# One store queue and seven v buffers in the first stage of a convolution and attention network (one core, fp32)

## The reference, cut to what matters

```python
g = group_norm(x)                         # 32 groups of 4 channels, per image
xn = g / (norm(g) * 128 ** -0.5 + 1e-8)   # simple_rms, per token
u = silu(xn @ W_u.T + b_u)                # made in a later stage, from the stored xn
v = silu(xn @ W_v.T + b_v)                # 256 channels: made and stored in the first stage
out = (u * conv2d_by_fft(v)) @ W_o.T + b_o + g
return x + out
```

## Time and profile before

| | |
|---|---|
| median of 3 runs | 3128.38 us (3125.18 to 3130.5) |
| the profiled execution, its own time | 3134.22 us |
| its span | 3132.4 us |
| busy in the span | TensorE 91%, VectorE 62%, ScalarE 40%, GpSimd 27% |
| moved | 315.48 MB, 101 GB/s mean |
| first stage over the images | about 21 to 331 us of the span |
| in that stage from 61 us on | TensorE busy 205.8 of 270 us, DMA share 0.77, 216 GB/s, mean granted TensorE clock 0.80 |

### The profile page before, as it was taken

One profiled execution on the slowest core, in us unless ns is written; L12 is line 12 of the kernel. 1 busy time (PEld: TensorE's weight loads), 2 busy tenths in 40 slices (PEclk: granted clock), 3 DMA queues, 4 the chain that ended last, 5 costly groups with the idle time before them and its releaser, 6 DMA issues. The chain is left out here.

```text
span 3132.4 us, 145347 instructions
## 1 busy us (share of the span) xinstructions
PE 2862.5 (91%) x62769; PEld 2113.4 (67%) x62769; DVE 1933.0 (62%) x3276; ACT 1262.5 (40%) x2841; POOL 843.7 (27%) x921
## 2 busy tenths in 40 slices
PE   5778798999999999999999979679999999999889
PEld 4555248966666666666666634348888888888779
DVE  4444353366666666666666657557778887778533
ACT  3555344332222222222222244356666666666300
POOL 0000002012222222222222212225555555555410
PEclk9778698999999999999999999889999999999999
DMA  5778100012112111212121199546666667666556
GB/s 139 213 211 231 53 1 1 0 31 46 45 44 46 44 46 44 46 44 46 44 46 44 43 366 400 228 80 104 106 102 99 100 105 107 102 103 98 80 142 199
DMA packets 839362, 315.48 MB, mean 101 GB/s; under 512 B 671729, under 2 KB 824878, under 8 KB 835118
## 3 DMA queue, kind: packets, MB, share of 16 engines
q1 hardware_dynamic: 503186, 176.24, 23.9%
q10 hardware_dynamic: 321692, 130.88, 15.8%
q0 software_dynamic: 14336, 6.45, 3.7%
HBM read 157.66 MB, written 155.75 MB: 100 GB/s over the span
## 5 line engine op out<-in xcount | busy, mean ns | idle before, releaser
L845 DVE TENSOR_TENSOR terms<-spec,ps_z 112x456 f32<-112x456 f32 x1024 | 575.0, 623 | 404.3 <-PE ps_z L728 404.3
L738 PEld LDWEIGHTS ps_q<-inv_w,prod 112*57 112x57 f32 x16384 | 450.9, 133 | 174.5 <-issue 172.2
L826 POOL TENSOR_TENSOR prod<-terms 112x456 f32<-112x456 f32 x256 | 297.6, 1162 | 1000.5 <-DVE terms L845 1000.5
L738 PE MATMUL ps_q<-inv_w,prod 112*57 112x56 f32 x16384 | 484.4, 217 | 1.2 <-DVE prod L851 1.2
L783 ACT ACTIVATE q_half<-ps_q 121x448 f32<-121x448 f32 x255 | 139.2, 546 | 827.1 <-PE ps_y L746 827.1
L728 PE MATMUL ps_z<-x_half,fwd_w 120*112 120x456 f32 x1024 | 458.4, 570 | 0.0
L1135 POOL TENSOR_TENSOR k_blocks<-k_mixed,same_of 128x896 f32<-128x896 f32 x112 | 188.1, 1680 | 398.2 <-ACT k_mixed L1301 398.2
L1152 POOL DMA_DIRECT2D v_blocks<-v_heads x448 | 272.7, 615 | 41.7 <-PE ps_o L1222 23.5
L728 PEld LDWEIGHTS ps_z<-x_half,fwd_w 120*112 120x112 f32 x1024 | 160.4, 176 | 122.0 <-issue 106.1
L1222 PE MATMUL ps_o<-p_norm,v_blocks 128*64 128x64 f32 x6272 | 213.4, 227 | 26.5 <-DVE p_norm L1386 23.6
L1222 PEld LDWEIGHTS ps_o<-p_norm,v_blocks 128*64 128x64 f32 x6272 | 197.4, 141 | 36.0 <-DVE p_norm L1386 29.8
(11 more groups left out here) (136 smaller groups left out, 4505.7 us busy)
## 6 DMA issues: line engine op xcount, KB each, us to landing
qk_heads<-st_qk ACTq DMA_DIRECT2D x56, 476.0 KB
qk_rows<-qk_heads SPq DMA_DIRECT2D x112, 238.0 KB
conv_in<-v_sb ACTq DMA_DIRECT2D x112, 224.0 KB, 3.3
v_in<-conv_in SPq DMA_DIRECT2D x512, 49.0 KB
conv_out<-y_sb ACTq DMA_DIRECT2D x512, 49.0 KB
y<-conv_out SPq DMA_DIRECT2D x8, 1792.0 KB, 13.2
x_in<-in_x SPq DMA_DIRECT2D x8, 1568.0 KB, 9.5
shortcut<-short ACTq DMA_DIRECT2D x8, 1568.0 KB, 6.2
```

Source lines behind the costliest of these rows:

```text
L738: last = pe.matmul(ps_q[64 * ri:64 * ri + NF, c * SIDE:(c + 1) * SIDE], prod[b % 2][:, x, c * NF:(c + 1) * NF], k.inv_w[:, x, ri * SIDE:(r ...
L826: pool.tensor_tensor(prod[b % 2][:, 1, :], terms[b % 2][:, 2, :], terms[b % 2][:, 3, :], ALU.add).then_inc(prod_i_r, 1)
L845: last = dve.tensor_tensor(terms[b % 2][:, x, :], k.spec[0:NFFT, s, bass.ds(c * CC, CC), :].rearrange("p c f -> p (c f)"), ps_z[b % 2][z][ ...
```

## The change

It is made in `project_in`, and one number in `attend`.

- `v_sb` gets NCH = 7 buffers in place of 2, one for each chunk of an image, with seven semaphores `v_stored`. The SiLU of chunk c of image b waits until the stores of chunk c of image b - 1 have landed.
- ScalarE issues no DMA in the stage any more. SyncE issues them all, loads and stores, from a program without a loop, in the order: loads 0, 1, 2; `short` of image 0; load 3; then for each image b the 14 stores of v, the store of `xr`, the store of `short` of image b + 1, and the load of image b + 4. Each waits for the same data as before; the load of image b still waits for image b - 2 to be turned.
- The increments of `aligned` ahead of TensorE's loop in `attend` go from 81 to 83.

TensorE's and VectorE's code in the stage is unchanged. The diff (the parts that only rename are in it too):

```diff
--- before.py
+++ after.py
@@ -218,7 +218,7 @@
         sq = [sb(f"x_sq{n}", [128, COLS]) for n in range(2)]
         rt, rt_eps, rinv = sb("rt", [TT, NCH * TPC]), sb("rt_eps", [TT, NCH * TPC]), sb("rinv", [TT, NCH * TPC])
         ROWS = COLS // SIDE
-        v_sb = [sb(f"v_sb{n}", [128, 2, ROWS, SIDE]) for n in range(2)]
+        v_sb = [sb(f"v_sb{n}", [128, 2, ROWS, SIDE]) for n in range(NCH)]
         gs = GroupStats(ctx, nc, "gn0")
         ps_ss = psum("ps_sumsq")
         ps_t, ps_bc, ps_v = ([psum(f"{n}{m}") for m in range(2)] for n in ("ps_turn", "ps_bcast", "ps_v"))
@@ -227,7 +227,8 @@
         sq_ready, ss_ready, rt_ready, eps_ready = sem("sq_ready"), sem("ss_ready"), sem("rt_ready"), sem("eps_ready")
         rinv_ready, bc_ready, xr_ready = sem("rinv_ready"), sem("bc_ready"), sem("xr_ready")
         v_ps_ready, v_ready, copies_read = sem("v_ps_ready"), sem("v_ready"), sem("copies_read")
-        v_stored, xr_stored, short_stored = ([sem(f"{n}{m}") for m in range(2)] for n in ("v_stored", "xr_stored", "short_stored"))
+        xr_stored, short_stored = ([sem(f"{n}{m}") for m in range(2)] for n in ("xr_stored", "short_stored"))
+        v_stored = [sem(f"v_stored{n}") for n in range(NCH)]
         block = ctx.enter_context(nc.Block())
 
         def cols(c):
@@ -248,13 +249,36 @@
 
         @block.sync
         def _(sp):
-            with sp.Fori(0, BATCH // 2) as i:
-                for a in range(2):
-                    b = i * 2 + a
-
-                    sp.wait_ge(x_turned, b * NCH + NCH)
-                    src = t.x_rows[bass.ds(b * TOK, TOK), :]
-                    sp.dma_start(x_in[a][:], src.rearrange("(a p) c -> p a c", p=TT)).then_inc(x_loaded[a], 16)
+            def load(b):
+                sp.wait_ge(x_turned, b * NCH + NCH)
+                sp.dma_start(x_in[b % 2][:], t.x_rows[b * TOK:(b + 1) * TOK, :].rearrange("(a p) c -> p a c", p=TT)).then_inc(x_loaded[b % 2], 16)
+
+            def store_short(b):
+                sp.wait_ge(short_ready, (b + 1) * NCH)
+                sp.dma_start(t.S[b], short[b % 2][:]).then_inc(short_stored[b % 2], 16)
+
+            def store_v(b, c):
+                sp.wait_ge(v_ready, (b * NCH + c) * 2 + 4)
+                for h in range(2):
+                    dst = t.V[b, c * ROWS:(c + 1) * ROWS, h * 128:(h + 1) * 128, :]
+                    sp.dma_start(dst.rearrange("r c w -> c r w"), v_sb[c][:, h]).then_inc(v_stored[c], 16)
+
+            def store_xr(b):
+                sp.wait_ge(xr_ready, b * NCH + NCH + 1)
+                sp.dma_start(t.XR[b], xr[b % 2][:]).then_inc(xr_stored[b % 2], 16)
+
+            for b in range(3):
+                load(b)
+            store_short(0)
+            load(3)
+            for b in range(BATCH):
+                for c in range(NCH):
+                    store_v(b, c)
+                store_xr(b)
+                if b + 1 < BATCH:
+                    store_short(b + 1)
+                if b + 4 < BATCH:
+                    load(b + 4)
 
         @block.tensor
         def _(pe):
@@ -295,27 +319,19 @@
         def _(act):
             act.sem_inc(x_copied, 2)
             act.sem_inc(v_ready, 2)
+            for n in range(NCH):
+                act.sem_inc(v_stored[n], 32)
             for n in range(2):
-                act.sem_inc(v_stored[n], 32)
                 act.sem_inc(xr_stored[n], 16)
                 act.sem_inc(short_stored[n], 16)
 
             def body(b, a, turn, norm, project):
                 def silu(c):
-                    n = (a * NCH + c) % 2
-
-                    act.wait_ge(v_stored[n], (b - a) * (NCH * 16) + ((a * NCH + c) // 2 + 1) * 32)
+                    act.wait_ge(v_stored[c], b * 32 + 32)
                     for h in range(2):
                         act.wait_ge(v_ps_ready, (b * NCH + c) * 2 + h + 1)
-                        act.activation(v_sb[n][:, h].rearrange("p r w -> p (r w)"), ps_v[h][:, 0:COLS], ACT.Silu,
+                        act.activation(v_sb[c][:, h].rearrange("p r w -> p (r w)"), ps_v[h][:, 0:COLS], ACT.Silu,
                                        bias=k.bias[:, 2 + h:3 + h]).then_inc(v_ready, 1)
-
-                def store(c):
-                    n = (a * NCH + c) % 2
-                    act.wait_ge(v_ready, (b * NCH + c) * 2 + 4)
-                    for h in range(2):
-                        dst = t.V[bass.ds(b, 1), c * ROWS:(c + 1) * ROWS, h * 128:(h + 1) * 128, :]
-                        act.dma_start(dst.rearrange("b r c w -> c (b r) w"), v_sb[n][:, h]).then_inc(v_stored[n], 16)
                 if turn:
                     act.wait_ge(copies_read, b + 3)
                 for c in range(NCH + 2):
@@ -328,23 +344,17 @@
                         act.wait_ge(xg_ready, (b + 1) * NCH + c + 1)
                         act.wait_ge(ss_ready, (b + 1) * NCH + c + 1)
                         act.activation(sq[c % 2][:], xg[1 - a][:, cols(c)], ACT.Square).then_inc(sq_ready, 1)
-                    if c > 1 and project:
-                        store(c - 2)
                 if turn:
                     gs.on_scalar(act, b + 2)
                 if norm:
                     act.wait_ge(ss_ready, (b + 2) * NCH + 2)
                     act.activation(rt[:], ps_ss[0:TT, 0:NCH * TPC], ACT.Sqrt, scale=1.0 / CH).then_inc(rt_ready, 1)
-                    act.wait_ge(short_ready, (b + 2) * NCH)
-                    act.dma_start(t.S[bass.ds(b + 1, 1)].rearrange("b p t -> (b p) t"), short[1 - a][:]).then_inc(short_stored[1 - a], 16)
-                if project:
-                    act.wait_ge(xr_ready, b * NCH + NCH + 1)
-                    act.dma_start(t.XR[bass.ds(b, 1)].rearrange("b p t -> (b p) t"), xr[a][:]).then_inc(xr_stored[a], 16)
             images(act, body)
             for n in range(2):
                 act.wait_ge(xr_stored[n], 16 * (BATCH // 2 + 1))
                 act.wait_ge(short_stored[n], 16 * (BATCH // 2 + 1))
-                act.wait_ge(v_stored[n], 32 * (BATCH * NCH // 2 + 1))
+            for n in range(NCH):
+                act.wait_ge(v_stored[n], 32 * (BATCH + 1))
 
         @block.vector
         def _(dve):
@@ -1238,7 +1248,7 @@
                     outputs(i - 1, (j - 1) % RING)
 
 
-            for _ in range(81):
+            for _ in range(83):
                 pe.sem_inc(aligned, 1)
             for w in range(AU):
                 for x in range(2):
```

## The result

The kernel after takes **3101.13 us** (median of 4 runs, 3099.78 to 3101.67), the kernel before 3127.45 us (4 runs, 3125.18 to 3130.5). The ratio is 0.9914, with a 95% interval of 0.99 to 0.9928: 26.3 us less. 3094.7 was forecast, with a range of 3083 to 3109. The profiled executions differ by 32.6 us in their spans, 3132.4 and 3099.8; of that 31.4 lie in the first stage, whose successor issues its first load at 300.34 in place of 331.72 us, and 1.2 behind it.

A forecast was written before the change was run, and what follows sets the result against it. TensorE was taken as the bound inside bodies, paying in full for ScalarE's store wait once per image. Gains of 31.3 (waits) + 2.4 (last body) = 33.7 us against the median 3128.4 gave 3094.7 us, range 3083 to 3109.

The forecast's parts named there:

- The waits: At the first stage's body ends, TensorE's waits for `rinv` fall from 47.3 to 16.0 us, a gain of 31.3 us.
- All in one queue: All first-stage transfers on SyncE's queue: 29.5 us an image with a load, 22.6 without; price 0.
- v: 3.21 MB at 219 GB/s: Time for one image's v stores in the first stage's queue: 14.7 us.
- The queue just keeps up: SyncE's queue keeps pace with the first stage's bodies; a store may be a whole body late unfelt; price 0.
- the last body's step: The first stage's data ends near +29.1 us from the last body's start; gain 2.4 us, ends 0 and 3.7.
- second rival: One queue is slower than two, v at 181 GB/s, 10 us paid behind the last body: 3105 us, chance 0.10.
- 7 us of a body's 30: SyncE's 17 issues of about 0.4 us in each first-stage body; price 0.
- The clock: TensorE's clock still falls around each first-stage body's end, so each body still pays about 4 us.
- first rival: TensorE's clock stays up in the first stage, bodies about 25.4 us, queue the bound: 3073 us; chance, wholly or partly, 0.12.
- none late: Bound on the clock term: TensorE's clock comes back late in none of the first-stage bodies, -4 us.
- falling up to 3 us into a body: Bound on the clock term: TensorE's clock falls only that far into a first-stage body, -5 us over six.
- bad loop: The loop in `attend` lies badly and TensorE waits 33 times: 39 to 109 us less 33.7, upper 3204 us, chance 0.05.

The follow-up runs named there:

- e1: The kernel before with seven v buffers and nothing else, ScalarE still issuing all stores: 3122.17 us, ratio 0.9985.
- e2: The kernel after with two v buffers again, all stores still on SyncE: 3127.53 us, ratio 0.9995.
- e3: The kernel after without the stores of `short` for images 1 to 7: 3089.08 us, ratio 0.9884.
- e5: The kernel after with `conv_in` laid out as image, channel, row, column, so v is stored in runs of 1792 bytes: 3084.24 us, ratio 0.9868.
- e7: The kernel after with 81 increments of `aligned` in place of 83: 3103.98 us, ratio 0.9931.
- e4: The kernel after with the stores of `xr` and `short` issued by ScalarE on its own queue: 3102.49 us, ratio 0.9928.
- e9: The kernel after with the second half of each chunk of v stored by ScalarE on its own queue: 3092.88 us, ratio 0.9889.

## Why the prediction was right, and where it was not

*The waits.* Right in size, and in mechanism for the two parts together. 16.0 us were to remain behind the first start's 1.7, 15.8 do: 2.1 to 2.2 at the ends of bodies 0 to 5, 2.8 at body 6. The step "What is late next is the roots' table load behind the last SiLU" is what the timeline after shows.

*The parts' shares.* The forecast never split the gain between the buffers and the move, and its wording, in which the SiLU "waits for stores of the image before", made the buffers the cause. e1 and e2 show that alone they are worth 3.8 us and the move nothing. The reading of the earlier trace rows was wrong by the issue of 3.87 us: it stood in the trace before, ahead of the SiLU, and the prediction counted the issues only as the 1.20 us ahead of the table load.

*All in one queue: the step that failed.* "v: 3.21 MB at 219 GB/s" is the top of a pulse of two or three stores, not a pace; kept busy the queue moves 187. The measured need is 25.4 to 25.7 us for an image without a load, where 22.6 were put, and 32.1 (183.97 to 216.07) with one, where 29.5 were. "The queue just keeps up" is wrong: bodies of 28.4 to 29.6 us are shorter than 32.1, it fell behind, and the stage paid for it behind the last SiLU, 23.9 us to the next load in place of the 8 that the last body's step gives. It is the second rival's mechanism, with its 181 GB/s, and as that rival said, no SiLU ever waited for it. e3 and e5 show it from two sides: with less in the queue, or the same in larger runs, the end comes 13.6 and 16.8 us earlier. The issues cost more than "7 us of a body's 30" too, 19 to 29 us of SyncE's time for the 14 stores of a body, but nothing waited for SyncE itself.

*The clock.* It fell around the ends of bodies 0 to 5 with only 2.2 us of rest there, as was argued from the earlier trace rows, so the first rival is out as a whole. At the end of body 6 it did not fall, with 2.8 us of rest, so body 7 ran warm throughout; of that rival's "runs in which it stays up in some bodies" this is one case. The clock also cost less than was left in: the bodies were to be 29.2, 31.5, 29.7, 31.8, near 29.5 twice and, by its work of 25.0 and rest of 2.8, 27.8 for body 6, and from TensorE's first instructions after they are 28.7, 29.6, 28.4, 29.6, 28.4, 29.6 and 25.4 (body 7 starts at 259.96), 9.3 us less in all:

```profile
118.55 0.65 PE L295 MATMUL ps_bcast<-ident,rinv 112*128 112x112 f32 x4 [2.13 <-DVE rinv L395]
146.96 0.98 PE L295 MATMUL ps_bcast<-ident,rinv 112*128 112x112 f32 x4 [2.21 <-DVE rinv L395]
259.96 0.98 PE L295 MATMUL ps_bcast<-ident,rinv 112*128 112x112 f32 x8 [2.81 <-DVE rinv L395]
...
257.00:262.00 5.00, 1.76 (x11) 1.22 (x11) 1.66 (x4) 2.24 (x4) 0.00 (x0) 1.00 0.89 182
```

In bodies 2 and 4 the first four broadcasts take 0.65 us, so the clock falls only after the body has begun, and in no body does it come back more than 10 us after the start; of the bounds named for this, "none late" came true, and "falling up to 3 us into a body" in bodies 2, 4 and 6. The third row has eight broadcasts in 0.98 us, and the stretch around it (the last line) has a granted clock of 1.00. The Trainium skill, "TensorE: Matmul & The Clock Gate", section "HAM oscillation — how this bites in real kernels", makes idle gaps the cause. The trace disagrees: with 2.2 us idle the clock fell, with 2.8 us it stayed. What differs is the time from one wide product to the next, 7.3 to 7.8 us at the ends of bodies 0 to 4, 6.2 at body 5 and 4.2 at body 6. That isn't the whole of it either, for in e5, with the same 2.8 and nearly the same 4.2 us, the clock fell for some 4 us at the start of body 7. What decides is open.

*How the number came out.* The stage's end was forecast at 298 and is at 300.3: body 7 begins 10.0 us sooner (0.8 of it from ahead of body 0), its SiLUs are done 16.5 us from its start and not near 20, and the queue costs 15.9 more behind them. That two errors of this size nearly cancel is luck. By the medians the gain is 26.3 us and not 33.7, for another reason: the prediction says that nothing in the sum hangs on the profiled execution's 5.8 us above the median. Something does. Before, the end moved with the clock's chance (331.7 and 320.7 in two executions); after, the queue fixes it. So the stage gains 31.4 us against the one execution of before and 20.4 against the other, and a difference taken against the slower one and then set against the median is too large. Set against its own execution the forecast was 3100.5.

*The other rivals.* The bad loop is out: nothing waits per pass, and e7 with 81 increments is 3 us from after. The Trainium skill's "DMA: Bandwidth & Descriptors", section "Issuing engines are not separate DMA queues", says more issuers bring no bandwidth: e4 agrees (300.27 against 300.34), e9, with 293.15, does not wholly.

## What to carry to other kernels

A wait for a buffer, an issue that takes long and a queue's backlog can all come from the same slow transfers. Take one of them away and the next holds the engine, so two parts of a change that gain almost nothing alone can gain a good deal together, and what the queue still lacks is paid behind the last instruction. In the trace, look what stood on the engine's own queue during a wait before putting all of it down to a semaphore. Cost a queue that will be kept full by its pace over steady work (here the 8 us with nothing but v in it), not by the peak of a pulse. Where a tensor is written in small runs by a stage whose DMA engines are full and read by one where they are a quarter busy (a share of 0.27 in the convolution, before and after), move the small runs to the reader: here that was worth 17 us, and 43 with the rest.

## What the runs showed of the hardware that I had not expected

Stores in runs of 224 bytes moved 187 GB/s from one queue and 190 from two, with a DMA share of 0.90 in the one and 1.32 in the other, so the share did not tell how much was left. It is above 1 with one queue too: 1.02 over 61 to 298 us of after, where SyncE's queue carried all of the stage. An issue behind other transfers can hold its engine, 3.78 us for two in e1 and 9.98 us for four on SyncE in e2, where an issue takes 0.38 us at its shortest in before. And the same program, with waits for `rinv` of 49.0 and 48.0 us, placed its TensorE clock so differently that one stage ended 11 us apart in two executions.
